# Three cross-attentions of a decoder: loops over pairs of batches written out

## What is computed

```python
x = x + _L0_xattn_ref(_layernorm(x), ctx_1024, mask, ...)   # 16 heads of 16
x = x + _L0_ffn_ref(_layernorm(x), ...)                     # experts, top 2
x = x + _L1_xattn_ref(_layernorm(x), ctx_1024, ...)         # relu attention
x = x + _L1_ffn_ref(_layernorm(x), ...)                     # self-attention, experts
x = x + _L2_xattn_ref(_layernorm(x), ctx_1024, ...)         # 16 heads of 64
x = x + _L2_ffn_ref(_layernorm(x), ...)                     # experts, top 1
x = x + _L3_xattn_ref(_layernorm(x), ctx_1024, ...)         # 16 heads of 64, with biases
x = x + _L3_ffn_ref(_layernorm(x), ...)                     # experts, dense
```

## Time and profile before

| what | us |
|---|---|
| median of 3 runs | 4162.86 (4162.65 to 4162.91) |
| profiled execution, its own time | 4161.14 |
| its span, first to last instruction | 4159.3 |
| TensorE (PE) busy | 3536.1 (85%) |
| VectorE / ScalarE / GpSimd busy | 1574.0 / 1536.9 / 1197.4 |
| mean granted TensorE clock | 0.923 of full speed |

### The profile page before, as it was taken

The page is one execution under the profiler, slowest core; times in us unless marked ns, Lnnn a source line. Parts: engine busy times, 40 slices in busy tenths (PEclk is TensorE's granted clock), DMA queues, the critical chain, the costliest instruction groups (busy, mean ns, idle before and its releaser), DMA issues. The chain is left out here.

```text
span 4159.3 us, 67079 instructions
## 1 busy us (share of the span) xinstructions
PE 3536.1 (85%) x22014; PEld 2897.3 (70%) x22014; DVE 1574.0 (38%) x3464; ACT 1536.9 (37%) x4297; POOL 1197.4 (29%) x1312
## 2 busy tenths in 40 slices
PE   5999992996897873975999999759599999997999
PEld 4777772885565652654889888658488888885665
DVE  3555552001225541014444544300344444444444
ACT  2333330432224550212555555324255444551111
POOL 0000003002000002014666666410466656661000
PEclk9999995998898976987999999779799999997999
DMA  3000002886110003331000000077200000000001
GB/s 117 12 11 11 11 1 82 304 309 211 51 34 4 0 2 106 116 112 34 9 7 9 9 7 5 3 241 280 74 10 9 9 9 9 8 1 12 23 19 33
DMA packets 102019, 240.30 MB, mean 58 GB/s; under 512 B 24682, under 2 KB 73644, under 8 KB 84012
## 3 DMA queue, kind: packets, MB, share of 16 engines
q1 hardware_dynamic: 94188, 219.82, 16.1%
q0 software_dynamic: 7680, 18.36, 1.7%
HBM read 208.78 MB, written 29.36 MB: 57 GB/s over the span
## 5 line engine op out<-in xcount | busy, mean ns | idle before, releaser
L642 POOL TENSOR_SCALAR L_probs<-L_probs,L_inverse 112x375 f32<-112x375 f32 x512 | 645.2, 1260 | 86.9 <-issue 86.9
L752 DVE TENSOR_REDUCE L_negmax<-bank 112x1 f32<-112x375 f32 x768 | 417.5, 544 | 559.7 <-PE bank L441 344.6
L608 ACT ACTIVATE L_probs<-bank,L_negmax 112x375 f32<-112x375 f32 x768 | 439.4, 572 | 407.1 <-DVE L_negmax L752 407.1
L464 PEld LDWEIGHTS bank<-ident,L_probs 112*125 112x125 f32 x2304 | 360.4, 189 | 108.3 <-ACT L_probs L608 47.1
L640 POOL TENSOR_TENSOR L_inverse<-L_sums,neg_one 112x1 f32<-112x1 f32 x512 | 315.2, 616 | 349.7 <-ACT L_probs L608 344.1
L464 PE MATMUL bank<-ident,L_probs 112*125 112x112 f32 x2304 | 376.0, 271 | 22.0 <-issue 10.3
L596 ACT ACTIVATE L_probsT<-bank 125x336 f32<-125x336 f32 x512 | 231.3, 452 | 315.4 <-PE bank L464 313.3
L479 PE MATMUL bank<-L_probsT,v 125*64 125x112 f32 x3072 | 206.1, 270 | 1.1 <-ACT L_probsT L596 1.1
L453 PE MATMUL bank<-L_kT,L_q 128*112 128x375 f32 x512 | 203.5, 478 | 0.0
L437 PE MATMUL bank<-L_keys_hi,L_q_hh 128*112 128x376 f32 x512 | 184.3, 360 | 8.9 <-DVE L_keys_lo L695 6.5
L581 ACT ACTIVATE v<-bank 125x512 f32<-125x512 f32 x192 | 114.9, 598 | 197.3 <-PE bank L391 197.3
(11 more groups left out here) (272 smaller groups left out, 7070.5 us busy)
## 6 DMA issues: line engine op xcount, KB each, us to landing
L0t_w<-in_F_w SPq DMA_DIRECT2D x70, 1024.0 KB, 5.1
L2t_w<-in_F_w SPq DMA_DIRECT2D x42, 1024.0 KB, 5.2
L_ctxT<-in_ctxT SPq DMA_DIRECT2D x48, 375.0 KB, 3.4
L1t_w<-in_F_w SPq DMA_DIRECT2D x16, 1024.0 KB, 6.2
slots_in<-zeros SPq DMA_DIRECT2D x4, 1792.0 KB, 16.5
L1x_ctxT<-in_ctxT SPq DMA_DIRECT2D x16, 375.0 KB, 3.0
L0t_xs<-slots_in SPq DMA_DIRECT2D x35, 128.0 KB, 6.0
L0t_b<-in_F_b SPq DMA_DIRECT2D x35, 128.0 KB, 6.1
```

The source lines that it names most:

```text
L464: ins = pe.transpose(psT[h % len(psT)][0:SJ, j * T:(j + 1) * T], probs[h % NB][:, j * SJ:(j + 1) * SJ], core.ident[0:T, 0:T])
L608: act.activation(probs[h % NB][:, :], psS[h % 2][0:T, 0:S], ACT.Exp, bias=negmax[b.par][:, h:h + 1], accum_out=sums[b.par][:, h:h + 1]).th ...
L642: pool.tensor_scalar(probs[h % NB][:, :], probs[h % NB][:, :], inverse[b.par][:, h:h + 1], None, ALU.mult)\
L752: dve.tensor_reduce(negmax[b.par][:, h:h + 1], psS[h % 2][0:T, 0:S], AX, ALU.max, negate=True).then_inc(maxed.sem, 1)
```

## The change

The loops over pairs of batches in the three cross-attentions are replaced by Python loops that write the same code out once per batch. Each wait's threshold is then a constant. The order of the work on every engine stays what it was, no operation on data is added or left out, and no buffer is changed. The three edits are in `run` (all four compute engines), in SyncE's loading of the context, and in GpSimd's part for L0.

```diff
             first(Batch(0, 0))
             heads(Batch(0, 0), True, False)
-            with engine.Fori(0, (B - 4) // 2) as i:
-                heads(Batch(i, 1), False, False)
-                heads(Batch(i, 2), False, False)
-            heads(Batch(0, B - 3), False, False)
+            for n in range(1, B - 2):
+                heads(Batch(0, n), False, False)
             heads(Batch(0, B - 2), False, False, False)
             heads(Batch(0, B - 1), False, True, False)
             tail(Batch(0, B - 1))
...
                     load_wide(Batch(0, 0))
                     next_ctx(Batch(0, 1))
-                    with sp.Fori(0, (B - 2) // 2) as i:
-                        next_ctx(Batch(i, 2))
-                        next_ctx(Batch(i, 3))
+                    for n in range(2, B):
+                        next_ctx(Batch(0, n))
                     return
                 load(Batch(0, 0))
                 load(Batch(0, 1))
-                with sp.Fori(0, (B - 2) // 2) as i:
-                    for k in (2, 3):
-                        b = Batch(i, k)
+                for n in range(2, B):
+                        b = Batch(0, n)
...
-                rstd(Batch(0, 0))
-                with pool.Fori(0, B - 1) as i:
-
-                    pool.wait_ge(var_ready.sem, var_ready.at(i + 2))
-                    pool.tensor_tensor(stats[:, 9:10], stats[:, 8:9], core.neg_half[0:T, :], ALU.pow)\
-                        .then_inc(rstd_ready.sem, 1)
+                for n in range(B):
+                    rstd(Batch(0, n))
```

## The result

| | us |
|---|---|
| kernel before, median of 4 | 4162.75 (4156.43 to 4162.91) |
| changed kernel, median of 4 | 4114.34 (4112.12 to 4125.81) |
| ratio of the two | 0.9893, interval 0.9872 to 0.9913 |
| profiled execution of the changed kernel, time / span | 4113.81 / 4112.0 |

The account below looks back on a forecast made before the run. It took TensorE to set the pace, with L3's loop stalling on instruction fetch at each way back. Gains of 31.8 (L3) + 0 (L2) + 1.4 (L0) = 33.2 us off 4162.86 gave 4129.7 us, range 4126 to 4142.

Parts of the forecast that it names:

- The stall, L3: TensorE in L3: removing five ways back, each stalling on code fetched again, saves 5 x 6.36 = 31.8 us.
- L2, nothing: TensorE in L2: looped and written-out passes both take 91.26 us, so the gain is nothing.
- L0, 1.4 us: TensorE in L0: twelve looped batches each get 0.12 us shorter when written out, 1.4 us in all.
- Added blocks: Instruction blocks on queue 8 rise from 108 to 138 at no cost; upper bound 2.3 us.
- Rival 3: Written-out code stalls at block borders, 2.1 us each in L0 and L2: 97 us more, 4227 us; 2 in 100.
- Rivals 1, 2 and 4: 1: L3 stall not way back's, 4161.5 us, 5 in 100; 2: part stays, about 4143, 5 in 100; 4: Rival 4.
- Rival 4: Another loop, such as layer 0's tile loops, is moved and starts to stall: +102 us, 4231 us; 2 in 100.
- The step that failed: Whole kernel: 33.2 us off the profiled execution's 4161.14, with the median 1.7 us above it, gives 4129.7 us.
- The range: Whole kernel: measured time between 4126 and 4142 us, the upper end near the gain of L3's branches alone.

Follow-up runs that it names:

- e1: The kernel before, unchanged, run and profiled again: 4155.82 us, ratio 1.0002 to the kernel before.
- e17: The kernel before, unchanged, once more against itself on one chip: 4158.99 us against 4153.51.
- e4: The kernel before with all loops kept and 32 more TensorE instructions (waits long met) ahead of L3's loop: 4124.14 us, ratio 0.9926.
- e13: The kernel before, loops kept, with TensorE waits added: 169 instructions ahead of L2's loop and 24 per batch inside it: 4177.83 us, ratio 1.0051.
- e14: Control for e13: the same 24 instructions per batch in L2, but 33 ahead of its loop: 4128.17 us, ratio 0.9933 to the kernel before.
- e2: The changed kernel, unchanged, run and profiled again: 4122.49 us, ratio 0.9924 to the kernel before.
- e11: The changed kernel, unchanged, against the kernel before on one chip: 4115.22 us, ratio 0.9903.
- e15: The changed kernel, unchanged, compared once more with the kernel before: 4121.11 us, ratio 0.9916.
- e6: The kernel before with VectorE's, ScalarE's and GpSimd's loops written out, except GpSimd's own in L0; TensorE's and SyncE's loops kept: 4153.37 us, ratio 0.9994.
- e7: The kernel before with only TensorE's loop in L0 written out: one execution, 4124.45 us.
- e12: The kernel before with the loops of e6 written out, TensorE looped, and 32 more TensorE instructions ahead of L3's loop: 4129.08 us, ratio 0.992.
- e5: The kernel before, loops kept, with 183 more TensorE instructions (waits long met) ahead of L2's loop: 4136.42 us, ratio 0.996.
- e10: The kernel before, loops kept, with 241 more TensorE instructions (waits long met) ahead of L3's loop: 4148.81 us, ratio 0.9976.

## Why the prediction was wrong, point by point

- **The stall, L3.** Right that it is the way back and its fetch, and right in size: 31.8 us forecast, 31.7 measured in the first pair, and batches at 47.1 us. That the two agree within 0.1 us is luck; L3 of the kernel before took 760.9 and 760.2 us in e1 and e17, which makes it 30.7 and 30.0. Clock 1.00, the waits on issue gone, as said. Wrong in the reason why L3 and not L2: the forecast has L3's body fetched again as "a little longer". e4 keeps the length and has no stall, and L2's still longer body stalls in e13 and not in e14: where the body lies decides.
- **L2, nothing.** Right: 709.2 before, and 708.9, 707.9 and 707.6 us in e2, e11 and e15. The 710.4 of the first profile came before batch 1.
- **L0, 1.4 us.** Right in size (561.1 to 559.7), wrong in the engine: I put it under TensorE, and e6 and e7 show that it is the other engines'.
- **Added blocks.** 138 forecast, 138 counted, and no cost seen: batches in L3 and L2 keep the period of those written out before. Rival 3 is out: under L0 and L2 too no batch got longer.
- **Rivals 1, 2 and 4.** L3's gain came whole, and the changed kernel has no stall at a border or in another loop (its longest branch on TensorE takes 0.23 us). Rival 4's mechanism is real, though. e13 made it, at 49.7 us, in a loop some 30 instructions longer than L3's.
- **The step that failed** is the one that made the sum into a time: "The median of the runs lies 1.7 us above that execution, so the forecast is 4162.86 - 33.2". It took the three executions of before, which lie within 0.26 us, for the spread of the kernel, and every stage outside the attentions for a constant. The runs showed this in its place: the kernel before has since taken 4145.93 to 4170.41 us in the comparisons' own executions, and its untouched self-attention 270.5 to 277.4 us in three profiles. The stages outside the attentions gave 15.4 us in the first pair of profiles, about the 15.4 us by which 4114.34 lies below the forecast. On the other occasions the medians differ by 31.9, 42.7 and 32.4 us.
- **The range** held the terms' bounds and nothing for what the sum leaves out. Two of the changed kernel's four medians lie below it by more than 10 us, the other two, 4122.49 and 4121.11, by 3.5 and 4.9: the starting point was high as well, by 4 to 9 us against the later medians of before.

Open: whether the mean of 38.9 us against 33.1 is chance; why e12's median is 13.9 us above e11's; what in a profile would foretell the self-attention's clock; and whether e5 stalls in some executions.

## What to carry to other kernels

A long hardware loop, here of some 1580 instructions of TensorE, can be fast or slow by where it lies: look at the closing branch's time (0.2 us or over 3) and at blocks on the instruction queue in later passes. Writing it out removes the stall; no cost of the written-out code was seen here. A few dozen instructions ahead of the loop can remove it too, but only until the code above changes: e7 lost the stall by a change to another attention, and e13 made one. Near the border one profile is not enough: compare it with the times of the other executions. Three equal times are no spread: before a forecast turns a sum into a time, see how much the stages outside it differ between executions.

## What the runs showed of the hardware

- A way back to a block that is gone costs 3.5 to 8.2 us, whatever its branch takes: 6.3 in L3 of before (31.7 us on five; the branch 4.2), 8.2 in e13 (753.2 - 712.1 on five; the branch 3.4), and 3.5, 4.0 and 5.9 in e10 (the branches 4.6 to 4.8). Part of it is the clock. In L3 of before a second block was waited for and the clock fell to half (0.51, rows 5) behind the standstill; e10's three stalled passes take 97.7, 98.2 and 100.1 us at 1.00, 0.98 and 0.97, against 94.2 at 1.00 without a stall.
- The border is sharp: of e10's five ways back, three stalled and two did not, with the same code. That fits a race between the jump and the request for the block behind the loop. The arrivals of the blocks above agree with it; the request itself is in no trace.
- The Trainium skill, page "Runtime: NRT & Kernel Launch", section "Instruction fetch mechanics", describes blocks of 256 instructions and room for 2048 on TensorE. L3's body has some 1580 by the program's count, 1579 in the trace of one pass. e4 agrees that the size would fit: no block on queue 8 in its passes 2 to 6. e13 and e14 add that a body of about that size fits only in some places: 43 blocks and none.
